# Small sums of the norm statistics on GpSimd in the first layer, and the row sends spread over four slots

## The reference

```python
def _L0_gnn_ref(node_feats, adj_matrix, W_lin, b_lin, W_q, W_k, ln_g, ln_b):
    X = _heads(lrelu(node_feats @ W_lin + b_lin), B, N)      # 4 heads of 32
    q = _heads(lrelu(node_feats @ W_q), B, N)
    k = _heads(lrelu(node_feats @ W_k), B, N)
    att = jax.nn.sigmoid(jnp.einsum('bhxd,bhyd->bhxy', q, k) * scale)
    adj_h = adj_matrix[:, None] * att
    deg = jnp.sum(adj_h, axis=-1)
    dis = jnp.where(deg > 0, deg ** (-0.5), 0.0)
    A = dis[..., :, None] * adj_h * dis[..., None, :]
    Y = jnp.einsum('bhxy,bhyd->bhxd', A, X)
    ...
    return (Y - mu) * jax.lax.rsqrt(var + LN_EPS) * ln_g + ln_b
...
x = x + _L0_gnn_ref(_layernorm(x, axis=-1), adj, ...)
x = x + _L0_ffn_ref(_layernorm(x, axis=-1), ...)     # top 2 of 8 experts for each token
```

## Time and profile before

| | |
|---|---|
| median of 3 runs | 731.24 us (729.73 to 732.97) |
| the profiled execution, its own time | 729.19 us |
| its span in the profile | 727.5 us |
| PE busy over the span | 631.1 us (87%) |
| DVE busy | 542.8 us (75%) |
| ACT busy | 470.6 us (65%) |
| POOL busy | 311.3 us (43%) |
| the first layer | 0 to about 305 us of the span |

### The profile page before, as it was taken

One profiled execution on the slowest core, in us unless ns is written; L12 is line 12 of the kernel. 1 busy time (PEld: TensorE's weight loads), 2 busy tenths in 40 slices (PEclk: granted clock), 3 DMA queues, 4 the chain that ended last, 5 costly groups with the idle time before them and its releaser, 6 DMA issues. The chain is left out here.

```text
span 727.5 us, 18525 instructions
## 1 busy us (share of the span) xinstructions
PE 631.1 (87%) x5438; PEld 528.6 (73%) x5438; DVE 542.8 (75%) x2478; ACT 470.6 (65%) x1284; POOL 311.3 (43%) x365
## 2 busy tenths in 40 slices
PE   3787998889888877789999999996889699999992
PEld 1454555555555545769999999995778687999992
DVE  7899999999999989734444444444999941778898
ACT  2778888888888754236676667662267747676660
POOL 1012322736455466725455454545632115756530
PEclk9999999999999999979999999999999979999996
DMA  5339232324222110536554554315994001022121
GB/s 156 102 110 183 74 103 74 103 81 139 70 78 76 58 40 28 167 122 165 135 123 113 148 145 135 104 56 108 174 268 144 27 1 60 24 65 59 31 67 50
DMA packets 75844, 72.15 MB, mean 99 GB/s; under 512 B 7793, under 2 KB 64818, under 8 KB 74978
## 3 DMA queue, kind: packets, MB, share of 16 engines
q1 hardware_dynamic: 61954, 50.28, 24.7%
q0 software_dynamic: 11200, 13.35, 7.5%
q10 hardware_dynamic: 2592, 7.34, 3.7%
HBM read 44.39 MB, written 26.55 MB: 98 GB/s over the span
## 5 line engine op out<-in xcount | busy, mean ns | idle before, releaser
L1483 ACT ACTIVATE hT<-psum,b1blk 128x128 f32<-128x128 f32 x364 | 104.1, 369 | 53.3 <-PE psum L1420 53.2
L1596 POOL DMA_INDIRECT expert_outputs<-y_rows,y_at x91 | 87.3, 959 | 96.8 <-DVE y_rows L1569 93.1
L1420 PE MATMUL psum<-xinT,w1blk 128*128 128x128 f32 x728 | 97.8, 278 | 1.1 <-ACT xinT L1473 1.1
L1441 PE MATMUL psum<-f_w,hT 128*128 x728 | 96.3, 276 | 0.0
L1420 PEld LDWEIGHTS psum<-xinT,w1blk 128*128 128x128 f32 x728 | 89.7, 194 | 2.0 <-ACT xinT L1473 1.3
L1126 POOL TENSOR_TENSOR y_n<-y_n,ln_g 128x256 f32<-128x256 f32 x30 | 22.3, 744 | 157.8 <-DVE gate L877 97.8
L1441 PEld LDWEIGHTS psum<-f_w,hT 128*128 128x128 f32 x728 | 88.4, 192 | 0.1
L1550 DVE TENSOR_SCALAR w1blk<-f_w 128x256 f32 x182 | 46.9, 299 | 46.2 <-issue 43.4
L823 DVE TENSOR_TENSOR adj_h<-psum,adjT 128x1024 f32<-128x1024 f32 x64 | 75.1, 1215 | 0.7 <-ACT psum L608 0.7
L608 ACT ACTIVATE psum<-psum 128x1024 f32<-128x1024 f32 x64 | 64.1, 1007 | 14.3 <-PE psum L358 14.3
L1139 POOL DMA_INDIRECT pair_rows<-rows,row_of x64 | 62.5, 977 | 17.9 <-issue 17.6
(11 more groups left out here) (318 smaller groups left out, 1450.5 us busy)
## 6 DMA issues: line engine op xcount, KB each, us to landing
adj_in<-in_adj_dram SPq DMA_DIRECT2D x32, 256.0 KB, 3.5
adjT_scratch<-adjT SPq DMA_DIRECT2D x32, 256.0 KB, 3.0
adjT<-adjT_scratch SPq DMA_DIRECT2D x6, 1024.0 KB, 5.1
xin<-pair_rows SPq DMA_DIRECT2D x91, 64.5 KB, 2.2
b2wide<-b_of_blocks ACTq DMA_DIRECT2D x10, 512.0 KB
xres<-in_x_dram SPq DMA_DIRECT2D x16, 256.0 KB, 3.3
xres<-expert_outputs POOLq DMA_DIRECT2D x6, 512.0 KB, 9.6
out_dram<-yout SPq DMA_DIRECT2D x6, 512.0 KB, 3.5
```

What stands on the lines that cost most here:

```text
L1420: ins = nc.tensor.matmul(psum[:, 2 + u, lo:lo + P], w1blk[:, u, k, c * P:(c + 1) * P], xinT[:, u, :], start=True, stop=True)
L1441: ins = nc.tensor.matmul(psum[:, 6 + n % 2, 0:D], hT[:, u, k, c, :], flat[:, bass.ds(places[k] + (HID + c * D), D)], start=(k == 0 and c = ...
L1483: ins = nc.scalar.activation(hT[:, u, k, c, :], psum[:, 2 + u, lo:lo + P], ACT.Gelu, bias=b1blk[:, c, k, n:n + 1])
L1596: pool.indirect_dma_start(y_dram[:, :], bass.IndirectOffsetOnAxis(ap=y_at[:, n % Y_AT:n % Y_AT + 1], axis=0), y_rows[:, u, :], None).then_ ...
```

## The change

In slots 1 to 31 GpSimd makes `mdiff`, `sqsum`, the square of `mdiff`, the scaled `sqsum` and, last, `msum`, at the head of its slot (`sums_of_stats`). It waits for the statistics and for the last solve (`s_norm`). VectorE's solve begins with an empty step, waits for four of the five in the next step, where it makes `veps`, and waits for the fifth before `shift`. In the other slots and in the drain VectorE makes them itself, in five instructions in place of four. The sends of groups 0 to 3 are spread: two tiles in each of the four slots behind the ranking. Group 4, ranked in slot 29, keeps its order of four tiles in slots 30 and 31.

```diff
@@ -246,7 +246,8 @@
         s_gate, s_ranked = sem("s_gate"), sem("s_ranked")
         s_stats, s_norm, s_chA, s_init1 = sem("s_stats"), sem("s_norm"), sem("s_chA"), sem("s_init1")
         s_x1 = sem("s_x1")
-        s_poolc = sem("s_poolc")
+        s_poolc, s_sums = sem("s_poolc"), sem("s_sums")
+        SUMS = 5
 
         KQ_BANK, AT_BANK, YT_BANK, Y_BANK = 4, 5, 6, 7
 
@@ -274,6 +275,9 @@
 
         def solves(s):
             return batch(s + 4) or batch(s - 1) or batch(s - 3) or batch(s - 5)
+
+        def stats_by(s):
+            return sum(TB for i in range(FIRST, s + 1) for b in (i + 5, i - 2, i - 4) if batch(b))
 
         def chooses(s):
 
@@ -751,21 +755,28 @@
                 was = (s - 1) % 2
                 mean_a, sq_a, mean_b, sq_b = (stats[:, was, :, i] for i in (1, 2, 4, 5))
                 v, r = veps[:, was, :], rstd[:, s % SETS, :]
-                dve.wait_ge(s_stats, stats_upto[s - 1])
+                if 0 < s < NB:
+                    assert stats_by(s - 1) == stats_upto[s - 1]
+                    yield
+                    dve.wait_ge(s_sums, SUMS * s - 1)
+                else:
+                    dve.wait_ge(s_stats, stats_upto[s - 1])
                 if batch(s - 1):
                     dve.wait_ge(s_degmax, s)
                 if solve_no(s) > 1:
                     dve.wait_ge(s_norm, 2 * solve_no(s) - 2)
-                chA.mark(nc.vector.tensor_tensor(msum[:, :], mean_a, mean_b, ALU.add))
-                chA.mark(nc.vector.tensor_tensor(mdiff[:, :], mean_a, mean_b, ALU.subtract))
-                chA.mark(nc.vector.scalar_tensor_tensor(sqsum[:, :], sq_a, EPS * D, sq_b, ALU.add, ALU.add))
-                yield
-                chA.settle()
-                chA.mark(nc.vector.scalar_tensor_tensor(mdiff[:, :], mdiff[:, :], 0.25 * STRETCH, mdiff[:, :],
-                                                        ALU.mult, ALU.mult))
-                yield
-                chA.settle()
-                chA.mark(nc.vector.scalar_tensor_tensor(v[:, 0:NLN], sqsum[:, :], STRETCH / D, mdiff[:, :],
+                if not 0 < s < NB:
+                    chA.mark(nc.vector.tensor_tensor(msum[:, :], mean_a, mean_b, ALU.add))
+                    chA.mark(nc.vector.tensor_tensor(mdiff[:, :], mean_a, mean_b, ALU.subtract))
+                    chA.mark(nc.vector.tensor_tensor(sqsum[:, :], sq_a, sq_b, ALU.add))
+                    yield
+                    chA.settle()
+                    chA.mark(nc.vector.tensor_tensor(mdiff[:, :], mdiff[:, :], mdiff[:, :], ALU.mult))
+                    chA.mark(nc.vector.tensor_scalar(sqsum[:, :], sqsum[:, :], STRETCH / D, STRETCH * EPS,
+                                                     ALU.mult, ALU.add))
+                    yield
+                    chA.settle()
+                chA.mark(nc.vector.scalar_tensor_tensor(v[:, 0:NLN], mdiff[:, :], 0.25 * STRETCH, sqsum[:, :],
                                                         ALU.mult, ALU.add))
                 yield
                 chA.settle()
@@ -803,6 +814,8 @@
                 chA.settle()
                 nc.vector.scalar_tensor_tensor(dis[:, s % SETS, :], v[:, NLN:NLN + NDEG], DEG_MIN * STRETCH,
                                                r[:, NLN:NLN + NDEG], ALU.is_gt, ALU.mult).then_inc(s_norm, 1)
+                if 0 < s < NB:
+                    dve.wait_ge(s_sums, SUMS * s)
                 nc.vector.scalar_tensor_tensor(shift[:, s % SETS, :], msum[:, :], -0.5, r[:, 0:NLN],
                                                ALU.mult, ALU.mult).then_inc(s_norm, 1)
 
@@ -1131,6 +1144,21 @@
                 pool.wait_ge(s_poolc, 2 * b + 3)
                 nc.gpsimd.tensor_tensor(xb, yn, xb, ALU.add).then_inc(s_x1, 1)
 
+            def sums_of_stats(s):
+
+                was = (s - 1) % 2
+                mean_a, sq_a, mean_b, sq_b = (stats[:, was, :, i] for i in (1, 2, 4, 5))
+                pool.wait_ge(s_stats, stats_by(s - 1))
+                pool.wait_ge(s_norm, 2 * solve_no(s) - 2)
+                nc.gpsimd.tensor_tensor(mdiff[:, :], mean_a, mean_b, ALU.subtract).then_inc(s_sums, 1)
+                nc.gpsimd.tensor_tensor(sqsum[:, :], sq_a, sq_b, ALU.add).then_inc(s_sums, 1)
+                pool.wait_ge(s_sums, SUMS * (s - 1) + 1)
+                nc.gpsimd.tensor_tensor(mdiff[:, :], mdiff[:, :], mdiff[:, :], ALU.mult).then_inc(s_sums, 1)
+                pool.wait_ge(s_sums, SUMS * (s - 1) + 2)
+                nc.gpsimd.tensor_scalar(sqsum[:, :], sqsum[:, :], STRETCH / D, STRETCH * EPS, ALU.mult, ALU.add)\
+                    .then_inc(s_sums, 1)
+                nc.gpsimd.tensor_tensor(msum[:, :], mean_a, mean_b, ALU.add).then_inc(s_sums, 1)
+
             def send(g, part):
                 if part == 0:
                     pool.wait_ge(s_rows, g + 1)
@@ -1142,13 +1170,17 @@
 
             def sends(s):
 
-                for r in (s - 2, s - 1):
+                for r in range(s - GB, s):
                     g = ranks(r)
-                    if g is not None:
+                    if g is not None and g < IN_DRAIN - 1:
+                        yield g, s - 1 - r
+                    elif g is not None and r > s - 3:
                         for part in (2 * (s - 1 - r), 2 * (s - 1 - r) + 1):
                             yield g, part
 
             for s in range(FIRST, NB):
+                if s > 0:
+                    sums_of_stats(s)
                 if batch(s - 4):
                     add_attention(s - 4)
                 for g, part in sends(s):
```

## The result

The kernel before and the changed one ran in turn on one chip, four times each. Before: 732.02 us median (729.73 to 732.97). Changed: **724.23 us** (720.03 to 726.62). The ratio is 0.9897, with a 95% interval of 0.986 to 0.9934, so the change is faster by 1.0%. The forecast was 725.0, in a range from 721 to 731.5. The profiled execution of the changed kernel took 725.08 us, its span is 723.1, and the granted clock over the span is 0.958 (before 0.971).

The account below looks back on a forecast made before the run. VectorE was taken to bound most slots, TensorE the ranking and early ones. Gains of 4.8, 1.35 and 0.5 + 0.4, minus 0.6 and 0.2, were summed to 6.2 us: 731.24 to 725.0 us, range 721 to 731.5.

Parts of the forecast that it names:

- VectorE's work and the new wait: In each slot VectorE's own work falls by 0.47 us, and its wait for GpSimd before `veps` is 0.2.
- the case with two stretches: Two GpSimd instructions beside `xs`, stretched 0.15 us each, put `veps` at 1.26 us after `shift` starts, 0.17 late.
- The sign that line 779 would wait above 1 us once: VectorE's idle time before `veps`, released by GpSimd: under 0.2 us on the mean, above 1 once, in slot 31.
- The case of full holding: Rival: GpSimd's five instructions and VectorE's hold each other, the wait is 0.8 us a slot; slower, 740 us; chance 12%.
- that of waits that eat the gain: Rival: GpSimd's chain puts `veps` at 1.56 us, a wait of 0.47; 730.8 us in all; chance 25%.
- The holding: GpSimd contends with VectorE instructions that have two SBUF inputs, such as `xs` and `veps`; seen before as 0.69 against 0.16 us.
- TensorE's floor: TensorE's own loop, 7.53 us a slot and 8.38 with ranking products, allows four slots no less than 30.97 us.
- The sign that went with the floor: VectorE's wait for TensorE's degrees would grow from 0.37 us and appear in more slots.
- Slots 2 to 6: These five early slots, bounded by VectorE, would gain 0.47 - 0.2 us each, 1.35 us in all.
- Slot 31: Its sums queue behind the four sends left in slot 30, and its gates come later: 0.6 us lost.
- What follows the first layer: The part behind the first layer would start earlier and stay as long.
- The sends: Two sends a slot instead of four take 2 x 1.27 us, ending well ahead of the next sums; no gain counted.

## Why the prediction was right, and where it was not

**VectorE's work and the new wait: right.** The forecast was 0.47 us less work in a slot and a wait of 0.2. Slot 2 without sums is 6.70 us against 7.11 before, 0.41 less, and the wait is 0.18 to 0.21. Three of the four groups came to 31.2 to 31.3 us and the last to 30.5; 31.2 was forecast. GpSimd's instructions took 0.20 by an estimate of 0.2, one step 0.17 by an estimate of 0.12, and `veps` was free 1.29 us behind the start of `shift` (176.84 to 178.13), where the case with two stretches had 1.26. The sign that line 779 would wait above 1 us once came twice, in slots 1 and 31. The case of full holding (0.8 a slot) and that of waits that eat the gain (0.47) did not come.

**The holding: right in kind.** Of the five instructions the scaled `sqsum`, which starts beside `xs` in most slots, is stretched, from 0.194 at its shortest to 0.381 at the median: 0.19 us. Where it ran clear of `xs`, as at 122.98 and 256.30, it took 0.20. `msum` under `veps` stayed at 0.21 at the median; once, beside `posk`, a pick with two SBUF inputs, it took 0.45. The Trainium skill, GPSIMD Engine Reference, section Key points, says that GpSimd contends with VectorE instructions that have two SBUF inputs. The trace agrees.

**TensorE's floor: the step that failed.** I wrote that line 408 in slots 7 to 9 "does not wait for `xd`", because no wait was marked at 87.45, and took 7.53 us as TensorE's own loop. This row of VectorE's timeline before stands beside it:

```profile
86.88 0.42 DVE L852 TENSOR_TENSOR xd<-psum,dis 128x256 f32<-128x256 f32 x1
```

`xd` ends at 87.30, and TensorE starts 0.15 behind that; at 159.56, the end of R, which I also called free, it is 0.15 behind the end of `xd` at 159.41. At 94.98 it is 0.15 again, and so it is, within 0.01, in each slot of the kernel before from slot 2 to 30. At these three places TensorE was waiting too, for less than the view marks. The changed kernel shows what a free start looks like; in slot 8, VectorE and then TensorE:

```profile
77.07 0.42 DVE L865 TENSOR_TENSOR xd<-psum,dis 128x256 f32<-128x256 f32 x1
77.96 0.60 PE L412 MATMUL psum<-ident,adj_in 128*128 128x128 f32 x4
```

`xd` ends at 77.49, 0.47 ahead of TensorE's line 412 (408 before), and TensorE works up to that line. The limit in those slots is 7.2 to 7.3 us, as the run without sums shows too, and R fell from 8.39 to between 8.01 and 8.07 as well; the last group, at 30.51, lies below the 30.97 that I had called a floor. Slots 7 to 9, forecast at nothing, gave 0.90. The sign that went with the floor failed too: VectorE's wait for the degrees at the end of R did not grow from 0.37 but fell to 0.30 to 0.32 in three groups and is unmarked in the other. The groups gave 0.83 more than forecast, all of it in the last two (1.56 and 1.74 where 1.2 was forecast).

**Slots 2 to 6: a term left out.** Of the 2.47 us, about 1.06 come from slots 5 and 6, where VectorE's squared difference took 0.69 instead of 0.16 beside GpSimd's first instruction of the residual add. I used the row for a cost of the change. It was also a cost of the kernel before, which the change removes: there is no such instruction on VectorE any more.

**Slot 31: mis-sized, minus 2.5 us for minus 0.6.** The forecast had the place and the cause. Counting from the gates before, at 265.36, hid what the slots ahead had gained. Slot 31 came 10.2 us earlier, but sends need their 5 us all the same, and the slot and the solve behind it cost 2.5: about 1.5 ahead of the gates, the wait for the sums, and 0.95 behind them, where the granted clock was 0.58 instead of 0.76; the forecast had no term for that stretch. Neither did it count slot 1, where no `xd` covers the chain, and VectorE waits 1.03 us.

**What follows the first layer: wrong.** "Starts earlier and stays as long" did not hold. The drain took 4.5 us longer, and TensorE's filler at a lower clock is the largest part of it that I can name. That the time was met is luck in part, by errors that cancel: up to slot 30 the gain was 10.7 us instead of 7.05, slot 31 and the start took 2.2 more than forecast, the drain another 4.5, and the rest of the program gave back 1.2. In the profiled executions 4.1 us are left (729.19 to 725.08), between the medians 7.8; the executions of the changed kernel lie 6.6 us apart, so the sum of 6.2 stands between two measurements that can't be told apart more finely here.

**The sends: priced at nothing.** On the first chip nothing speaks against that, but no run there has them alone. On chip A they are worth 2.6%, and the traces of B and C show the same lag behind sends.

**Open.** Why the same sends hold up the use of TensorE's results on three chips and not on the first; why the clock is lower in the drain after the change (with the last group's sends spread the 48 filler products still took 7.85 us, and in the kernel before on chip C they took 7.74, so on these chips it is not the change that slows them); what the wait for the sums in slot 31 costs by itself, since it occurs on the first chip alone; and what the filler's cut would bring on the first chip.

## What to carry to other kernels

No wait marked is not no wait: compare the start with the end of the instruction that it depends on, and where the gap is the same each time, it is a dependency. Work moved to an idle engine should be asked for as late as its chain allows; one place later in the order was worth as much on chip B as leaving the work out. A slot at the end of a pipeline, where that engine also has its transfers to issue, needs a sum of its own, from the time at which the slot will then begin.

## What the hardware showed that I had not expected

Four sends in a slot cost 1.9 to 3.9 us on chip C, against the same slots on the first chip, where `xh1T` does not start late beside them. The durations of single instructions are equal (most sends in a slot 0.95 to 1.02 us, `xd` 0.42), and so are the slots ahead of the first send. Chips A and B show the same lag. A small instruction on GpSimd costs 0.17 us from start to start between tensor_tensors, and 0.27 from a tensor_tensor to the tensor_scalar that waits for one two places back (177.48 to 177.75).
